# Zero fp32 products in front of the clearing products of the five gather passes of a graph-network kernel

## What is computed

```python
# layer 0, two graph convolutions
msg = norm[:, None] * h[src]
agg = jax.ops.segment_sum(msg, dst, num_segments=num_nodes)
# layer 1, attention (the "gat" pass)
e = scores_u[src] + scores_v[dst]
ex = jnp.exp(e - m[dst]);  s = jax.ops.segment_sum(ex, dst, num_segments=N_NODES)
agg = jax.ops.segment_sum(xh[src] * probs[:, None, :], dst, num_segments=N_NODES)
# layer 2, typed attention (the "hgt" pass), layer 3, a gated sum over the edges (the "l3" pass)
```

## Time and profile before

| | |
|---|---|
| three runs | 7785.73, 7786.81, 7802.5 us; median 7786.81 |
| profiled execution, its own time | 7788.46 us |
| its span, first to last instruction | 7786.7 us |
| mean granted TensorE clock over the span | 0.762 of full speed |
| instructions in the span | 118,192 |

### The profile page before, as it was taken

How to read it: one execution, slowest core, us unless ns; L and a number is a source line. 1 busy time by engine, 2 the same in 40 slices (tenths; PEclk the granted TensorE clock), 3 DMA queues, 4 the chain that set the end, 5 groups by cost and what they waited for, 6 DMA issues and landing times. The chain is left out here.

```text
span 7786.7 us, 118192 instructions
## 1 busy us (share of the span) xinstructions
PE 5059.6 (65%) x26286; PEld 3803.4 (49%) x26287; DVE 4681.0 (60%) x12672; ACT 3283.5 (42%) x7820; POOL 4933.0 (63%) x4975
## 2 busy tenths in 40 slices
PE   6777775666665677772555557865666665777774
PEld 4555654444454555551444444435555543555553
DVE  7666664555554777774445545436666566566666
ACT  0222221444444455440444434435666541655553
POOL 0677775777776777774777770037777700777774
PEclk6666566888887888885666668977877777898897
DMA  0222221222223122233666672457777722666665
GB/s 27 59 53 54 55 55 46 54 55 55 55 55 47 53 55 54 55 52 90 179 180 179 182 164 85 143 169 221 234 225 229 216 69 80 208 201 200 201 200 139
DMA packets 818177, 921.29 MB, mean 118 GB/s; under 512 B 120930, under 2 KB 657002, under 8 KB 817706
## 3 DMA queue, kind: packets, MB, share of 16 engines
q0 software_dynamic: 198144, 441.54, 22.6%
q1 hardware_dynamic: 403498, 368.52, 15.9%
q10 hardware_dynamic: 216320, 109.07, 4.8%
HBM read 724.85 MB, written 193.87 MB: 118 GB/s over the span
## 5 line engine op out<-in xcount | busy, mean ns | idle before, releaser
L783 POOL DMA_INDIRECT arena<-t,stage_idx x3328 | 3268.1, 982 | 1249.8 <-issue 992.8
L822 PE MATMUL ps<-arena 128*128 128x128 f32 (+2 forms) x8320 | 1801.7, 378 | 770.0 <-DMA arena<-t,stage_idx 640.3
L822 PEld LDWEIGHTS ps<-arena 128*128 128x128 f32 x8320 | 1581.2, 258 | 1036.3 <-issue 935.6
L831 DVE TENSOR_TENSOR arena<-arena,ps 128x512 f32 (+2 forms) x1040 | 835.2, 803 | 733.0 <-PE ps L822 666.9
L739 POOL DMA_INDIRECT d_rec<-arena x784 | 782.5, 998 | 438.7 <-issue 241.5
L2664 POOL DMA_INDIRECT arena<-t,stage_idx x832 | 831.7, 1000 | 297.0 <-issue 224.2
L819 PE MATMUL ps<-int_tmp 128*128 128x512 bf16 (+1 forms) x1664 | 554.5, 402 | 622.9 <-DVE arena L831 340.3
L1861 PE MATMUL ps<-arena 128*128 x2496 | 393.4, 295 | 584.5 <-DVE arena L2087 323.5
L1263 PE MATMUL ps<-arena 128*128 128x416 f16 x3328 | 721.5, 368 | 0.0
L1195 ACT ACTIVATE arena<-arena 128x128 f16<-128x128 f16 x1664 | 662.2, 480 | 6.9
L1861 PEld LDWEIGHTS ps<-arena 128*128 128x128 f32 (+1 forms) x2496 | 346.6, 204 | 642.1 <-issue 620.9
(11 more groups left out here) (445 smaller groups left out, 8254.2 us busy)
## 6 DMA issues: line engine op xcount, KB each, us to landing
spill<-arena ACTq DMA_DIRECT2D x208, 512.0 KB
arena<-spill SPq DMA_DIRECT2D x208, 512.0 KB
arena<-t,stage_idx POOLq DMA_INDIRECT x4160
arena<-d_loT SPq DMA_DIRECT2D x208, 256.0 KB
arena<-s_loT SPq DMA_DIRECT2D x104, 512.0 KB, 4.8
arena<-key_d SPq DMA_DIRECT2D x98, 512.0 KB
t<-arena SPq DMA_DIRECT2D x98, 512.0 KB, 3.0
d_rec<-arena POOLq DMA_INDIRECT x784
```

The source lines that it names most:

```text
L783: pool.indirect_dma_start(out=rows[r][:, i, :], out_offset=None, in_=table, in_offset=bass.IndirectOffsetOnAxis(ap=stage_idx[:, 8 * r + i: ...
L822: return nc.tensor.matmul(self.banks[i // 4][:, bass.ds(self.slot[i], self.width)], weights, rows, start=False, stop=False, skip_group_che ...
L831: nc.vector.tensor_tensor(at, at, got, ALU.add).then_inc(self.added, 1)
```

## The change

A method `clear_slowly(z, times)` takes the place of `clear(z)` in the five passes. It first issues `times` products of 128 x 128 zeros in fp32 with 512 columns (the same 128 columns of zeros read four times) into the first 512 columns of the part, then calls `clear(z)`. How many there are is in the table `SPARE`: two in c1 and one in c2 and l3, for z = 0 only; two in gat and one in hgt, for both z. In gat and hgt they are there only while gathers run: for the halves weighed after the loop over the windows `weigh.spare` is 0.

```diff
--- before.py
+++ after.py
@@ -121,6 +121,7 @@
         int_tmp = sb("int_tmp", P, I32)
         int_tmp2 = sb("int_tmp2", 1, I32)
         zeros16 = int_tmp[:, :].bitcast(BF16)
+        zeros32 = int_tmp[:, :].bitcast(F32)
         rank_hot = before[0:NT, 64:64 + NT]
         NUMBER_ROW = 96
         d_src = sb("d_src", SX, I32)
@@ -817,6 +818,13 @@
                 for y in range(4 * self.pitch // 512):
                     half = self.banks[z][:, 512 * y:512 * (y + 1)].rearrange("p (r f) -> p r f", f=self.pitch)
                     nc.tensor.matmul(half[:, :, 0:self.width], zeros16[:, 0:P], self.blank, start=True, stop=False, skip_group_check=True)
+
+            def clear_slowly(self, z, times):
+
+                for _ in range(times):
+                    wide = self.banks[z][:, 0:512].rearrange("p (r f) -> p r f", f=P)
+                    nc.tensor.matmul(wide, zeros32, bcast_mid(zeros32, 4), start=True, stop=False, skip_group_check=True)
+                self.clear(z)
 
             def product(self, i, weights, rows):
                 return nc.tensor.matmul(self.banks[i // 4][:, bass.ds(self.slot[i], self.width)], weights, rows, start=False, stop=False, skip_group_check=True)
@@ -1136,6 +1144,8 @@
         def underway(t):
             return not isinstance(t, int) or 0 <= t < DONE
 
+        SPARE = {"c1": 2, "c2": 1, "gat": 2, "hgt": 1, "l3": 1}
+
         def convolve(which, table, half_of, Nodes):
 
             new_stage()
@@ -1249,7 +1259,7 @@
                             sums.slots(pe, n)
                             for z in range(2):
                                 need(pe, sums.added, 2 * n + z - 1)
-                                sums.clear(z)
+                                sums.clear_slowly(z, (1 - z) * SPARE[which])
                                 if z == 0:
                                     pe.wait_ge(landed[r], base + 128 * k + 128)
                                 for i in range(4 * z, 4 * z + 4):
@@ -1883,7 +1893,7 @@
                             pe.wait_ge(den, n + 1)
                             sums.slots(pe, n)
                         need(pe, sums.added, 2 * n + s - 1)
-                        sums.clear(s)
+                        sums.clear_slowly(s, weigh.spare)
                         pe.wait_ge(msg, 2 * n + s + 1)
                         for i in range(4 * s, 4 * s + 4):
                             last = sums.product(i, at[:, b, i], m[:, b, i])
@@ -1921,7 +1931,9 @@
                             half(w, j)
                     if gat:
                         pe.wait_ge(split, 5)
+                    weigh.spare = SPARE[which]
                     windows(pe, body)
+                    weigh.spare = 0
                     v, left = WINDOWS - 1, HALVES - LAG
                     raise_window(v)
                     weigh(left, 0, 0)
@@ -2723,7 +2735,7 @@
                     sums.slots(pe, n)
                     for z in range(2):
                         need(pe, sums.added, 2 * n + z - 1)
-                        sums.clear(z)
+                        sums.clear_slowly(z, (1 - z) * SPARE["l3"])
                         pe.wait_ge(v_s, 6 * n + 3 * z + 3)
                         for i in range(4 * z, 4 * z + 4):
                             last = sums.product(i, at[:, b, i], rows[:, 8 * b + i, D:3 * D])
```

## The result

| | before | changed |
|---|---|---|
| median of 20 runs each | 7787.76 us | 7804.66 us |
| lowest and highest | 7779.43 to 7802.5 | 7797.0 to 7812.94 |
| profiled execution, its own time | 7788.46 us | 7806.39 us |
| its span | 7786.7 us | 7804.6 us |
| granted clock over the span | 0.762 | 0.821 |

The ratio is 1.0020, with a 95% interval of 1.0014 to 1.0027: 17 us slower (11 to 21), just over the 0.2% (15.6 us) that I had taken as the edge of no change. The forecast was 7787 us, the range 7762 to 7812. The range holds the result; the likeliest case does not quite, and the result lies where the rival of the meetings began.

What follows compares the result with a forecast made beforehand. POOL's stream of gathers was taken to bound every pass, with room for TensorE's added products. Tails of -5 us and long gathers of +6 us sum to +1, called 0: 7787 us, no change, range 7762 to 7812.

Steps and rivals of the forecast that it cites:

- the likeliest case: Whole kernel: no change, 7787 us, within 0.2% (15.6 us); chance 0.59.
- the rival of the meetings: All passes: DVE lengthens more gathers; one in three of 197 halves gives +27 us, 7814; decides from one in six; chance 0.17.
- POOL's stream of gathers sets the length of every pass: Five gather passes: POOL's busy time plus gaps of 0.30 us makes 5345 of their 5384 us.
- A product costs 0.91 us at the high level and 1.91 at the low one: All passes: 968 added products of two records cost TensorE 881 us at 2.4 GHz or 1849 us at 1.2 GHz.
- I take the high level: TensorE in the passes: dense new records raise the granted clock above 0.9, so all the added work fits.
- The new products stand before TensorE's wait for rows or messages, so take the place of idle time: Halves of the passes: new products fill TensorE's idle time before gathered rows or messages come; cost 0.
- In gat and hgt the tail has no new products, so 0: After the last gather of gat and hgt: no gain or loss, 0 us.
- Tails of c1, c2 and l3, -5 us: After those passes' last gathers: two groups of sums at the high clock save 1.8 us a pass, -5 us together.
- Long gathers, +6 us: All passes: faster TensorE moves DVE's meetings with POOL's gathers; one half in sixteen taken as lengthened, +6 us.
- l3: Pass l3, with only two buffers: delay of 0.1 us against 1.6 us of room; cost 0, between -9 and +9.
- TensorE becomes the bound (8032): gat and c1: if the clock doesn't rise, products exceed idle time, +205 and +40 us, 8032 us; chance 0.05.
- Faster (7761): Tails -5, POOL's waits on TensorE in l3 -9, fewer long gathers -12: -26, 7761 us; chance 0.19.

Runs made afterwards that it cites:

- doubled: The changed kernel with all counts of new products doubled (c1 4, c2 2, gat 4, hgt 2, l3 2): 7926.08 us against 7789.68, ratio 1.0170.
- tails_off_path: The kernel before, with 20 zero products behind the sums in each tail of gat and hgt: 7776.51 us against 7789.68, ratio 0.9983.
- the changed kernel with the two additions: The changed kernel plus two small DVE additions in c1 before each half's f16 instructions: 9880.76 us against 9696.18, ratio 1.0180.
- the tails with them: The kernel before, with zero products behind the sums in gat's and hgt's tails and two small DVE additions in c1: 9650.81 us, ratio 0.9945.

## Why the prediction was right, and where it was not

- **"POOL's stream of gathers sets the length of every pass": right.** The gaps are 0.30 us (996.4 us over 3270), the passes last 1066 to 1097 us, within the 1055 to 1100 foretold, and a clock from 0.62 to 0.79 in gat moved its length by nothing. The sum near zero rests on this, and this part of it held.
- **A product costs 0.91 us at the high level and 1.91 at the low one: right.** Four records take 1.88 and 3.78 us.
- **"I take the high level": half right.** The clock came to 0.89, 0.89, 0.79, 0.83 and 0.96, above 0.9 in one pass only, and a record of the new line took 0.57 us on average (1103.7 / 1936) over busy time, not 0.45. The step that failed is that the closer to busy, the more like the dense stage: the waits of 3.5 to 6 us between groups stay, and the first products behind one are at the low level. The Trainium skill ("TensorE: Matmul & The Clock Gate", section "A second HAM failure mode: psum-queue depth-cycling") describes such a swing between the two levels, from short idle gaps between groups of products. These rows show the swing (four new records take 3.58 us behind a wait of 6.04, and 1.88 us without one), with longer gaps, and no run here shows that it has the page's cause. Only in doubled did c1 reach 0.99, and that made nothing faster.
- **"The new products stand before TensorE's wait for rows or messages, so take the place of idle time": right in c1 and c2, wrong in gat and hgt.** I had looked it up in c1 and carried it over. In gat and hgt the messages are made before the bank is freed, so there is no wait left behind the clear. The trace of before had it: between the clear and the sums TensorE never waits in these two passes (no gap of over 0.1 us in 182 groups of each), while in c1 it waits in half of them, 355 us in all. It cost nothing inside the pass, for the reason given (POOL has room), so the term of 0 came out right there.
- **"In gat and hgt the tail has no new products, so 0": the step that failed.** It measured +8 us after gat and +5 after hgt, on average over the profiles (9.6 and 0.1 in the result's own pair). There are no products in the tail, but the lag that those of the last window leave is. I priced the delay at POOL alone, which has two halves of room while it gathers; after its last gather that room is what TensorE, SyncE's reload and DVE must work off. gat_ends_early takes the last window's products away, and gat's 8 us are gone. For hgt the lag is read from the traces, and no run takes its last products away.
- **Tails of c1, c2 and l3, -5 us: measured 0.** The gaps after the three passes are 25.7, 82.3 and 85.6 us, before 25.5, 82.5 and 85.5. The last halves wait for their rows behind the new products, and the clock is down again when these come:

```profile
2402.15 2.07 PE L830 MATMUL ps<-arena 128*128 128x128 f32 x8 [4.81 <-DMA arena<-t,stage_idx]
...
2408.74 1.96 PE L826 MATMUL ps<-int_tmp 128*128 128x512 f32 x4
2410.53 0.38 PE L820 MATMUL ps<-int_tmp 128*128 128x512 bf16 x1
2415.55 2.07 PE L830 MATMUL ps<-arena 128*128 128x128 f32 x8 [4.64 <-DMA arena<-t,stage_idx]
```

  The group of eight takes 2.07 us at the low level, as in before, although the products ahead of it ran at the high one. A product in front of such a wait, 4.6 to 4.8 us, warms nothing behind it.
- **Long gathers, +6 us: about right in size.** c1 +5.7 and c2 +2.8, on average over the profiles; c2's, and gat, hgt and l3, are within scatter. The share of one half in sixteen was a guess, so the match in size is luck. c1's mean gather went from 972 to 976 ns, the 4 ns that I had set as the mark. The rival of the meetings thus had the mechanism of up to half the loss. It came at a quarter of the +32 us that the rival counted. The rival's edge of one in six leaves out its own -5: with it the 15.6 us are reached at about one in five.
- **l3: right.** POOL's waits on TensorE there are 13.0 us (16.2 before), the pass within its scatter.
- **TensorE becomes the bound (8032): not in this dose.** doubled reaches that bound, by the count of products and not by a low clock (0.90 in gat): POOL waits for DVE behind TensorE, and the pass takes 92 us more. **Faster (7761)** asked for warm tails; tails_off_path got 7776.51 that way, and the change put no product where they could be had.

The forecast's terms with what was measured: c1 and c2 +8 instead of +6, tails 0 instead of -5, stretches after gat and hgt +13 instead of 0, gat and hgt themselves -4 (within scatter): +17, and the medians differ by 16.9. That it comes out so closely is luck, since the -4 is scatter, and l3 (+1) and the part before c1 (+2), left out here, are as large. What stands is that the 13 us I had put at nothing are most of the loss. The result lies in the range because the range was wide enough for the rival of the meetings, not because I had seen this.

## What to carry to other kernels

Work that is added to an engine with idle time is free only where something else still has to be waited for behind it: for each place, see which wait comes **last** in front of the useful work. A ring that absorbs a delay inside a loop gives it back when the loop ends, so the last turns are to be priced by themselves, and added work left out of them. To keep an engine's clock up, put the idle work behind the useful work, right up to the next wait's end, and only where that engine's speed is on the path; in front of a wait of 5 us it warmed nothing here.

## What the runs showed of the hardware

- Products of zeros raise the granted clock: from 0.62 to 0.79 in gat, and to 0.99 in c1 with four such products a half. A record of 128 x 512 in fp32 takes 0.46 to 0.47 us at the high level and 0.95 at the low one.
- A gather of 0.94 us on POOL beside a run of four f16 instructions on DVE is lengthened by an amount that depends on where in the gather the run starts. Over nine profiles, with the two gathers that follow: 0.71 us more at a start 0.10 to 0.15 us into the gather, about 0.11 at 0.20 to 0.35, 0.1 at 0.90, on average 0.33 at 1.15 (in the gap before the next, with a wide spread) and 0.16 at 1.25. DVE's fp32 messages do it too: in gat of the changed kernel 44 of the 49 gathers over 1.3 us are beside L2019, such as that of 1.44 us at 4656.22 above.
- In one session every kernel took about 25% longer, the stretches between the passes after gat and hgt left as they were, with gaps of 0.4 to 1.1 us between TensorE's instructions that no wait explains; the durations of single instructions were as usual. Before, the changed kernel with the two additions, and the tails with them came in the order that they have elsewhere, and their distances were larger.
